# Decoder layer on one core: projection and attention heads as one loop over 512 tokens, q and k moved from SBUF to SBUF

## The reference

```python
xn = rms(layernorm(x)) * g1
Q, K, V = (xn @ W.T for W in (Wq, Wk, Wv))     # reshaped to 16 heads of 16
pQ, pK = elu(Q), elu(K)
Q1, Q2 = split(pQ); K1, K2 = split(pK)         # 8 + 8 features of a head
kv1 = einsum('bshe,bshd->bsed', K1, V) * SCALE # per token, over its 16 heads
w1  = einsum('bshe,bsed->bshd', Q1, kv1)       # the same for Q2, K2 -> w2
attn = (1 - LAMBDA_INIT) * rms(w1 - lmb * w2, g2)
...                                            # rms with g3, a two-layer gelu block
```

## Time and profile before

| | us |
|---|---|
| median of 3 runs | 831.49 (829.99 to 834.1) |
| profiled execution, its own time | 828.94 |
| its span, first to last instruction | 827.2 |
| mean granted clock of TensorE | 0.851 |
| PE busy | 674.6 (82%), 8346 matmuls |
| DVE, ACT, POOL busy | 496.1, 359.2, 332.2 |

### The profile page before, as it was taken

The page is one execution under the profiler, slowest core; times in us unless marked ns, Lnnn a source line. Parts: engine busy times, 40 slices in busy tenths (PEclk is TensorE's granted clock), DMA queues, the critical chain, the costliest instruction groups (busy, mean ns, idle before and its releaser), DMA issues.

```text
span 827.2 us, 22126 instructions
## 1 busy us (share of the span) xinstructions
PE 674.6 (82%) x8346; PEld 624.3 (75%) x8346; DVE 496.1 (60%) x1237; ACT 359.2 (43%) x814; POOL 332.2 (40%) x393
## 2 busy tenths in 40 slices
PE   5784788577667746667646899999999999999998
PEld 4663667466556635657645799999999999999997
DVE  4752564222222247777835787777777777777763
ACT  4463464121112324443434555455555655545442
POOL 0131331000000098888623455555545545554323
PEclk9798899555555678776865999999999999999999
DMA  8466676655553123323410001111000101100000
GB/s 256 57 174 147 188 176 159 138 95 106 118 114 109 65 65 103 114 89 103 133 38 20 19 21 32 34 33 34 32 13 19 32 32 32 32 32 13 13 15 26
DMA packets 86567, 62.65 MB, mean 76 GB/s; under 512 B 30680, under 2 KB 83168, under 8 KB 86496
## 3 DMA queue, kind: packets, MB, share of 16 engines
q1 hardware_dynamic: 86496, 61.65, 28.8%
HBM read 36.47 MB, written 25.17 MB: 75 GB/s over the span
## 4 chain that ended last, share of the span: by engine, by line
PE 61%; issue 16%; DVE 11%; POOL 4%; DMA 4%; ACT 2%; SPq 1%; DVEq 0%; POOLq 0%; ACTq 0%
PE banks L602 43%; PE banks L714 5%; PE banks L732 4%; PE banks L747 3%; PE banks L655 2%; DMA h_qk<-qk_scratch 1%; POOL f_hT_lo L1667 1%; DVE m_t L1337 1%; PE banks L666 1%; DVE m_at L1330 1%; DVE m_n L1324 1%; DMA n_gw<-in_L_ffn_gate_w_dram 1%; DVE p_st L1231 1%; DVE p_xn L1244 1%; POOL m_rh L1578 1%
## 5 line engine op out<-in xcount | busy, mean ns | idle before, releaser
L1667 POOL TENSOR_TENSOR f_hT_lo<-f_hs,f_hT_hi 128x512 fp32r<-128x512 f32 x64 | 87.1, 1361 | 103.1 <-ACT f_hT_hi L1163 103.1
L1298 DVE TENSOR_TENSOR h_sm<-banks,blockmask 128x1024 f32<-128x1024 f32 x32 | 37.7, 1219 | 102.0 <-PE banks L714 102.0
L1578 POOL TENSOR_TENSOR m_rh<-m_ms,mhalf 128x32 f32<-128x32 f32 x16 | 88.3, 5519 | 1.3
L1530 DVE SCALAR_TENSOR_TENSOR f_hs<-banks,nbic,f_h 128x256 f32<-128x256 f32 x128 | 54.5, 478 | 43.0 <-PE banks L602 43.0
L602 PE MATMUL banks<-woT_hi,f_hT_lo 128*128 128x256 f32 x256 | 74.6, 291 | 0.2 <-POOL f_hT_lo L1667 0.2
L602 PE MATMUL banks<-f_adT_hi,lbT_lo 128*128 128x256 f32 x256 | 72.9, 285 | 0.1
L602 PE MATMUL banks<-woT_lo,f_hT_hi 128*128 128x256 f32 x256 | 71.9, 281 | 0.0
L602 PE MATMUL banks<-woT_hi,f_hT_hi 128*128 128x256 f32 x256 | 71.7, 280 | 0.0
L602 PE MATMUL banks<-f_xT_hi,wiT_lo 128*128 128x256 f32 x256 | 71.6, 280 | 0.0
L602 PE MATMUL banks<-f_xT_lo,wiT_hi 128*128 128x256 f32 x256 | 71.6, 280 | 0.0
L602 PE MATMUL banks<-f_xT_hi,wiT_hi 128*128 128x256 f32 x256 | 71.5, 279 | 0.0
(11 more groups left out here) (261 smaller groups left out, 2173.5 us busy)
## 6 DMA issues: line engine op xcount, KB each, us to landing
qk_scratch<-p_qk SPq DMA_DIRECT2D x32, 256.0 KB, 2.4
h_qk<-qk_scratch SPq DMA_DIRECT2D x32, 256.0 KB, 5.0
xin<-in_x_dram SPq DMA_DIRECT2D x8, 512.0 KB, 5.0
v_scratch<-p_v SPq DMA_DIRECT2D x16, 256.0 KB, 4.1
h_v<-v_scratch SPq DMA_DIRECT2D x16, 256.0 KB, 3.5
attn_scratch<-h_wn SPq DMA_DIRECT2D x16, 256.0 KB, 2.5
m_w<-attn_scratch SPq DMA_DIRECT2D x16, 256.0 KB, 2.7
m_x<-in_x_dram SPq DMA_DIRECT2D x16, 256.0 KB, 2.9
```

The source lines that it names most:

```text
L1298: dve.tensor_tensor(h_sm[:, r, 2 * s:2 * s + 2], pairs[s][:, :, :], blockmask[:, :].rearrange("p (o n) -> p o n", o=1).broadcast_to([P, 2, ...
L1530: ins = dve.scalar_tensor_tensor(out=f_hs[:, j % 2, c * T:(c + 1) * T], in0=bank[HB[j]][:, c * T:(c + 1) * T], scalar=nbic[:, f:f + 1], in ...
L1578: pool.tensor_tensor(out_ap, tmp, mhalf[:, 0:width], ALU.pow).then_inc(done, 1)
L1667: pool.tensor_tensor(lo, f_hs[:, j % 2], hi.bitcast(F32), ALU.subtract).then_inc(f_hlo, 1)
```

## The change

Stretches 2 and 3 become one loop of 8 units on every engine, laid out by a new `over_all`, which emits all steps one by one without a loop in the program. Everything after it stays. In detail:

- PE's step now holds, in this order (number: how many steps after its projection a unit gets there): values(0) 2, project_v(1) 1, turn_x(0) and (1) 0, values(1) 2, project(0) 0, turns 0, 1 and 2 2, project(1) and (2) 0, scores(0) 1, project_v(0) 0, project(3) 0, scores(1) 1, turn 3 2. The lists of ACT, DVE, POOL and SP are merged in the same way.
- The eight banks are now shared by both kinds of work: q and k go to banks 0, 6, 7, 7 (`QB`), v to bank 6, the turned x to 1 and 3, the turned heads to 1, 2, 7, 6 (`TB`). So PE waits more often for a bank to be read.
- p_xn, p_xT and the small tiles of the normalisation have one buffer where they had two.
- q and k no longer pass through DRAM. `tiles_in(b, i)` copies the piece of token group i from p_qk (128 partitions) to h_qk (16 partitions), 128 KB each: 4 for q (b = 0), 4 for k (b = 1) per unit, in place of 4 stores and 4 loads of 256 KB. A copy waits until the one before the last has landed, so two are in flight. The rows of h_qk thereby come in another order of heads; the columns of the v weights (`"values"`) and the choice in `head_turn` follow it.
- v still goes through DRAM scratch.
- The first `load_w` is issued after the last `store_w`. `turn_x` of unit 0 waits for all weights; the clearing of banks 4 and 5 moves to the start.

```diff
+def over_all(units, stages):
+    for t in range(units + max(lag for lag, _ in stages)):
+        for lag, emit in stages:
+            if 0 <= t - lag < units:
+                emit(Unit(0, t - lag, t - lag))
...
+        QB = (0, 6, 7, 7)
+        VB = 6
+        XB = (1, 3)
+        TB = (1, 2, 7, 6)
...
+            def tiles_in(b, i):
+                def emit(u):
+                    if i == 0:
+                        if b == 0 and u.has(2):
+                            sp.wait_ge(h_sd, nth(u, ROUNDS, -ROUNDS))
+                            apart(sp)
...
+                        sp.wait_ge(p_fin, nth(u, 4, 2 * b + 2))
+                        apart(sp)
+                    if i >= 2:
+                        sp.wait_ge(h_qkin[u.slot][i % 2], u.turn * 64 + 32 * b + 16)
+                        apart(sp)
+                    sp.dma_start(h_qk[32 * i:32 * i + HD, u.slot, H * b:H * b + H].rearrange("e h t -> e (h t)"),
+                                 p_qk[:, u.slot, KD * b:KD * b + KD, i * P:(i + 1) * P]).then_inc(h_qkin[u.slot][i % 2], 16)
+                return emit
...
-            over_units(sp, SU, [(0, but_first_two(load_x)), (1, heads_of(1)), (2, store_qkv), (2, heads_of(0))])
...
-            over_units(sp, SU, [(0, but_first_two(load_qk)), (0, but_first_two(load_v)), (2, with_last(start_mix, SU)), (4, store_w)])
+            over_all(SU, [(0, but_first_two(load_x))] + [(2, tiles_in(1, i)) for i in range(ST)] +
+                     [(2, store_v(0)), (2, store_v(1)), (2, load_v(0)), (1, tiles_in(0, 0)), (2, load_v(1))] +
+                     [(1, tiles_in(0, i)) for i in range(1, ST)] + [(3, store_w)])
...
+            first_two(load_w)
...
-            over_units(pe, SU, [(2, project(0)), (2, project(1)), (1, turn_x), (2, project(2)), (2, project(3)), (2, project_v(0)), (2, project_v(1))])
-            over_units(pe, SU, [(1, head_scores(0)), (2, head_values(1)), (3, head_turn(2)), (3, head_turn(3)),
-                                (1, head_scores(1)), (1, head_values(0)), (2, head_turn(0)), (2, head_turn(1))])
+            over_all(SU, [(2, head_values(0)), (1, project_v(1)), (0, turn_x(0)), (0, turn_x(1)), (2, head_values(1)),
+                          (0, project(0)), (2, head_turn(0)), (2, head_turn(1)), (2, head_turn(2)), (0, project(1)),
+                          (0, project(2)), (1, head_scores(0)), (0, project_v(0)), (0, project(3)), (1, head_scores(1)),
+                          (2, head_turn(3))])
...
+            over_all(SU, [(3, head_rows(1)), (1, p_exps(0)), (3, head_natural(0)), (3, head_natural(1)), (3, head_natural(2)),
+                          (1, p_exps(1)), (1, p_exps(2)), (1, p_values(0)), (1, p_exps(3)), (3, head_natural(3)),
+                          (2, head_rows(0)), (0, p_split(0)), (0, p_split(1)), (1, p_values(1))])
...
+            over_all(SU, [(2, p_elus(0)), (2, p_elus(1)), (2, p_elus(2)), (3, head_masked(0, 0)), (3, head_masked(0, 1)),
+                          (1, p_normalise), (1, prepare_rest), (2, p_elus(3)), (3, head_masked(1, 0)), (3, head_masked(1, 1)),
+                          (1, p_low(0)), (1, p_low(1)), (0, p_moments)])
...
+            over_all(SU, [(2, p_final(1)), (2, p_final(2)), (2, p_final(3)), (0, p_rstds), (1, p_final(0))])
```

More of the change, by code:

```diff
@@ L71, in has, with later @@
         return self.least >= back
-    def before(self, back):
-        return Unit(self.pair, self.offset - back, self.least - back)
+    def later(self, n, units):
+        return self.index + n < units
 def nth(u, per_unit, k, loops=0):
@@ L410, in from_bank @@
                 return turned.rearrange("p (c h e) -> p c h e", c=4, e=HD)
+            if at is not None and at[0] == "values":
+                return turned.rearrange("p (c h e) -> p c h e", c=2, e=HD)
             return turned
@@ L657, in turn, with turn_x, emit @@
                 return ins
-            def turn_x(u):
-                pe.wait_ge(p_norm, nth(u, 1, 1))
-                if u.has(1):
-                    pe.wait_ge(p_lo, nth(u, KD, 0))
-                for k in range(KD):
+            def turn_x(k):
+                def emit(u):
+                    pe.wait_ge(p_norm, nth(u, 1, 1))
+                    if u.has(2):
+                        pe.wait_ge(h_smd, nth(u, 2 * ROUNDS, -2 * ROUNDS))
+                    elif k == 0 and not u.has(1):
+                        pe.wait_ge(s_wlo, len(jobs))
+                        pe.wait_ge(s_foldlo, 3)
                     for i in range(ST):
-                        ins = pe.transpose(bank[k][:, i * P:(i + 1) * P], p_xn[:, u.slot, i, k * P:(k + 1) * P], identf[:, :])
+                        ins = pe.transpose(bank[XB[k]][:, i * P:(i + 1) * P], p_xn[:, i, k * P:(k + 1) * P], identf[:, :])
                     ins.then_inc(p_turned, 1)
+                return emit
             def project(c):
@@ L963, in _, with p_split, emit @@
             high_parts(len(jobs) - 2, len(jobs))
-            def p_split(u):
-                if u.has(2):
-                    act.wait_ge(p_vd, nth(u, 2, -2))
-                for k in range(KD):
+            def p_split(k):
+                def emit(u):
+                    if k == 0 and u.has(1):
+                        act.wait_ge(p_qkd, nth(u, 4, 0))
+                        act.wait_ge(p_vd, nth(u, KD, 0))
                     act.wait_ge(p_turned, nth(u, KD, k + 1))
-                    act.activation(p_xT[u.slot][0][:, k, :], bank[k][:, :], ACT.Copy).then_inc(p_hi, 1)
+                    act.activation(p_xT[0][:, k, :], bank[XB[k]][:, :], ACT.Copy).then_inc(p_hi, 1)
+                return emit
             def p_exps(c):
@@ L977, in emit @@
                         act.wait_ge(p_elud, nth(u, 4, c - 1))
-                    act.activation(p_exp[:, c % 2], bank[2 + c][:, :], ACT.Relu, scale=-1.0).then_inc(p_negd, 1)
+                    act.activation(p_exp[:, c % 2], bank[QB[c]][:, :], ACT.Relu, scale=-1.0).then_inc(p_negd, 1)
                     act.wait_ge(p_negd, nth(u, 4, c + 1))
@@ L1197, in low_parts @@
                         lo = target(dst[1], at)
[L1198 removed]
+                        parts = [(lo[:, c], turned[:, c], hi[:, c]) for c in range(4 if at[0] == "heads" else 2)]
                         for to, src, high in parts:
@@ L1263, in prepare_rest @@
             def prepare_rest(u):
-                if not isinstance(u.index, int) or u.index:
+                if u.index:
                     return
+                dve.wait_ge(s_foldc, 2)
+                for b in (4, 5):
+                    ins = dve.memset(bank[b][:, :], 0.0)
+                ins.then_inc(h_zeroed, 1)
                 dve.wait_ge(s_lamexp, 1)
@@ L1594, in emit @@
                     if c == 0 and u.has(2):
-                        pool.wait_ge(p_stored[u.slot], u.turn * 96)
+                        for k in range(2):
+                            pool.wait_ge(h_qkin[u.slot][k], u.turn * 64)
                     apart(pool)
```

205 lines of the change are left out of this document (102 added, 103 removed).

## The result

The changed kernel takes 800.02 us (median of 4 runs, 799.09 to 800.26), against 832.27 us for the kernel before on the same chip: a ratio of 0.9612, 95% interval 0.9585 to 0.9638. It is 32 us faster where 13.5 were forecast.

A forecast was written before the change was run, and what follows sets the result against it. Heads were taken as bound by instruction packets, projection by a 20 us stall. Steps of 26.4 + 1.8 + 0.8 = 29.0 us, six making 174, with fill and drain ended the stretch 13.5 us earlier: 818 us, range 794 to 838.

The forecast's parts named there:

- the clock term of a full step: PE's clock alternating in each step of the new loop: 5.3 of the 9.5 us between full and half clock.
- the stall: Projection before, 60 to 81 us: PE half busy while SP waits for unit 0's q, k, v; 20 us, called the gain.
- The start, to the first product: Fill of the new loop: turn_x of unit 0 starts at 33.5 us, first product at 36.8 in place of 33.82.
- The first two steps: Fill of the new loop: first step ends at 45.4 us, the second takes 18.3, to 63.7.
- my signs of being wrong: Profile after: PE waiting for elu, masks or h_wn over 3 us a step, or for h_qk, or clock at either level throughout.
- The work of a full step: PE's matmuls and transposes in a filled step: 21.1 us at full clock, 30.6 at half, 26.4 taken.
- The rival of the full clock: Clock stays full in the new loop: step 24.5 us, total 791; chance 0.14.
- the half clock: Rival: clock stays at half in the new loop and projection pays; step 32.6 us, total 840; chance 0.14.
- The gaps of the program's transport: PE waiting for instruction packets in scores(1), turn 3 and values(0): 1.8 us a step, ends 0 and 5.3.
- Handovers: PE's waits for banks in a step: 16 at 0.05 us, 0.8 us; 3 if the cover were gone.
- The copies of q and k: Direct 128 KB copies: 4 us each, bounds 2.7 and 4.9, hidden behind the step, nor a gain.
- The end: Drain: step nine 18 us to 255.7, step ten 13 to 268.7, then 4 more before m_sq, 272.7.

## Why the prediction was right or wrong

The step that failed is the clock term of a full step. I put it at 5.3 us a step, because I let the clock fall to half at the bursts of heads; it measured 1.5. Over six steps that is 22.8 us too much; the whole sum was 16.6 us too long, as other terms erred the other way. In place of the bursts, waits for instructions stood before each fall of the clock. A second claim failed with it: that the steady loop hardly gains, and that the stall is the gain.

**The start, to the first product: right.** `turn_x` of unit 0 begins at 34.2 (forecast 33.5), the first product at 37.5 (36.8).

**The first two steps: 8.1 us too short.** The first full step begins at 71.8, not 63.7. Of that 2.1 us stand already at the end of the first step (47.5, not 45.4), whose first ten products ran at half clock. In the second PE waited 6.0 us for q and k ahead of the first scores. The walk had "the load of x ahead" of the k copies and gave it no price. A wait of PE for h_qk was among my signs of being wrong; it came this once. DVE waited for x too, which I had ruled out, for 2.0 us in the six full steps and at no cost to PE. Moving that load brought 4.2 of the 8.1 us back. It is the same transfer that makes the long waits later, and both times I asked only whether x itself would be late.

**The work of a full step: 26.4 forecast, 127.2 / 6 = 21.2 measured.** Two sizes were off.
- *The pace of the values matmuls.* I took 2.34 us for 128 head matmuls at either clock, from the two scores rows. For scores that holds: 2.36 us at 168.89, at full clock. But the values, 64 rows of 64x64, take 1.58 us at 134.08, 12.3 ns each, against 1.10 / 60 = 18.3 ns at half clock. Both of a step together are 1.5 us cheaper, and the full-clock step is 19.7 us, as 200.6 to 223.05 shows, in place of 21.1. The rows of before could not show the values at full clock (those 5 us held scores only); I extended a measured equality to an operation that it had not been measured on.
- *The clock.* I took 5.3 us a step for it; it cost (127.2 - 6 x 19.7) / 6 = 1.5. Granted was 0.91, outside the 0.65 to 0.85 that I named. By my walk the clock would be down after each burst of heads, and half of the time. In the step from 200.6 on it is full throughout, with all four rounds of heads in it; where it falls, PE waits for instructions or has just done so (1.5 to 4.9 us), and it is back after 4 to 8 us. The gelu block, from which I took the half-way mean, was not a near pattern: PE is busy for 66% of it and for 84% here. That share alone does not decide it, as the kernel with half of the products is at 0.75, the mean that I had taken, with PE busy for 82%. The rival of the full clock (step 24.5, 791 us) was nearer to the truth than the forecast, and the half clock did not come. The Trainium skill (TensorE: Matmul & The Clock Gate, "Part 4: PE-mode transpose") says that transposes do not raise the clock. The half clock that I drew from it as a rival did not come. Either way 24 transposes a step lie here between products and the clock stayed up; no run here changes the transposes alone, so the rule was not put to the proof.

**The gaps of the program's transport: 1.8 us a step forecast, 4.0 measured.** The account by packets was right: 26.8 packets' worth of instructions in the stretch, 27 packets in the instruction queue, and the waits at borders of 256 instructions. What I left out is that these packets go through the same DMA engines as the data. With the load of x elsewhere the term is 14.5 / 6 = 2.4, near the forecast. The Trainium skill (Runtime: NRT & Kernel Launch, "Instruction fetch mechanics") has the fetch hidden; by the 24.1 us of PE waiting here it is not.

**Handovers: 0.8 forecast, nothing measured.** In the full steps PE never waited for DVE, ACT or POOL. The step walked held; with the products bunched, and so the cover of the masks gone, they cost 14.7 / 6 = 2.5 us a step, near the 3 that I had named for that, though as one wait and not as four short ones.

**The copies of q and k: 4 us forecast, 3.6 measured; "nor is it a gain" wrong.** They were hidden in the full steps, with no wait of PE for them. But the way through DRAM in this loop costs some 26 to 29 us (0.993 against 0.9612, or 828.6 against 800.0): SP stands still for landings of q and k 35 times in place of 19, for 84.5 us in place of 46.5, and SP's list is the bound then. I had costed the transfers on PE's clockwork and given SP's queue no sum of its own. With 67 us of waits and 20 more for POOL in 151, SP was not free in the changed kernel either. The Trainium skill (DMA: Bandwidth & Descriptors, "Anatomy of one DMA") would give an estimate of 2.3 us a copy. Its formula is a fit for copies that GpSimd issues, while SP issues these; 3.6 us with two in flight and 5.2 with four are measured.

**The end: right.** Step nine takes 18.9 us (18), from there to the first `m_sq` 14.1 (17). ACT waits 5.5 us for `m_w` where 4 were named. The last h_wn stands at 250.6, where 268 was named.

**The sum.** +8.1 for the first two steps, -22.7 for the six full steps, +0.9 and -2.9 for the end: 16.6 us under the forecast at the first `m_sq`, which stands at 256.1 and not at 272.7. It is 30.1 us earlier than in the kernel before, and the span 28.8 shorter. The measured time lies inside the range, but for other reasons than the ones given.

By step it is the same account: 25.2 us in place of 29.0, from 5.2 less work, 2.2 more gaps and 0.8 less handovers. Errors of both signs cancel in part, so the sum came out nearer than its terms.

**Where the gain was said to be.** "The gain is the 20 us stall": only in part. It was 15 us long, and taken away in the kernel before, it brings 8 to 10. "The steady loop alone hardly gains": it takes 25.2 us a unit, in place of 29.5. What was gained over projection and heads together can be read from PE. From the first `turn_x` to the first `m_sq` it was busy for 184.2 us and idle for 71.3 before; after, 178.2 and 43.7. So 27.7 us are idle time, 6.0 are busy time, and 3.6 are lost by the later start: 30.1. Of the idle time the waits for "issue" fell from 43.2 to 27.2 us. The higher clock in the steps (0.91 in place of 0.56) can show in the busy time only, so it brought 6 us at most: the products had run at full clock before as well, and the scores take the same time at either clock. What it did was to keep the products from becoming dearer inside the loop. How much each part of the change gives was not separated beyond what the runs above show, and they do not add up: the loop without the direct copies keeps only 6 us.

## What to carry to other kernels

Where matmuls are short and the profile shows waits for "issue" at every 256 instructions, treat the program as one more DMA stream: keep large transfers away from the moment when a burst of short matmuls needs its next packet (13 us here for moving one load on SP's list, 9 of them in the full steps and 4 at the start). Sum each DMA-issuing queue over a step like an engine, with every landing that it waits for; that sum decided here whether a loop brought 6 us or 32. Before a clock is forecast from a pattern, look at what PE did just before each fall of the clock: here it was a wait each time, and the products decided how long the clock stayed down. And a pace measured at both clocks for one shape of matmul says nothing of another.

## What the runs showed of the hardware

- Packets of instructions queue behind data: none was carried while 16 DMA engines were 97% busy for 5 us, and PE stood still for 4.9 us. With x half as large, the longest wait was 2.1 us, and in the step without a load of x 1.4.
- Matmuls of 16 rows by 64x64 take 18.3 ns each at either clock; those of 64 rows by 64x64 take 12.3 ns at full clock and 18.3 at half.
- With 36 matmuls of 128x512 among 512 short ones a step, the granted clock was 0.91 (0.83 to 0.96 in the other kernels with the same work in another order or with other transfers); with 18 of them 0.75; with the short ones almost alone, as before, 0.56. In the first of these (0.91) every fall of the clock came in a wait of PE (1.45 to 4.93 us) or within 2 us of its end.
- A copy of 128 KB from SBUF to 16 partitions of SBUF lands in 3.6 us with two in flight and 5.2 with four, and with four the DMA engines are busy 62% of the time in place of 54% for the same bytes.
